# The transposes of the masked LoRA values: from TensorE to VectorE

## What is computed

```
x = x + S4(x)                    # a long convolution, masked by a length
x = x + einsum(x, W1[cond])      # per-sample 32x32 channel mixes
x = x + einsum(x, W2[cond])
def lora_add(base, inp, A, B):
    t = einsum('bri,bni->bnr', A[idx], inp)
    return base + einsum('bor,bnr->bno', B[idx], t) * 0.5
gate = lora_add(x @ W_gate.T, x, A_gate, B_gate)
up   = lora_add(x @ W_up.T,   x, A_up,   B_up)
act  = silu(gate) * up
x = x + lora_add(act @ W_down.T, act, A_down, B_down)
```

## Time and profile before

| | us |
|---|---|
| median of 3 runs | 1084.07 (1083.23 to 1085.55) |
| the profiled execution | 1087.87 |
| its span, first to last instruction | 1086.1 |
| PE busy | 1054.7 (97%) |
| DVE, ACT, POOL busy | 264.7, 405.2, 484.8 (24%, 37%, 45%) |
| mean granted clock of PE | 0.997 of full speed |

### The profile page before, as it was taken

One profiled execution on the slowest core, in us unless ns is written; L12 is line 12 of the kernel. 1 busy time (PEld: TensorE's weight loads), 2 busy tenths in 40 slices (PEclk: granted clock), 3 DMA queues, 4 the chain that ended last, 5 costly groups with the idle time before them and its releaser, 6 DMA issues.

```text
span 1086.1 us, 18858 instructions
## 1 busy us (share of the span) xinstructions
PE 1054.7 (97%) x6136; PEld 928.8 (86%) x6136; DVE 264.7 (24%) x519; ACT 405.2 (37%) x627; POOL 484.8 (45%) x301
## 2 busy tenths in 40 slices
PE   3899899999999999999999999999999999999998
PEld 3665699888889899998898998999888889989997
DVE  8333112222222222222221222122222212221222
ACT  7002234434433443343344334333434433343341
POOL 0604355445445444545454454445454544544441
PEclk9999999999999999999999999999999999999999
DMA  9699442424333333424243333434242433334320
GB/s 342 220 397 333 127 115 92 133 59 140 92 111 101 104 108 101 120 85 133 64 135 97 108 99 99 119 100 117 83 133 69 135 94 105 100 99 123 102 74 20
DMA packets 100979, 135.49 MB, mean 125 GB/s; under 512 B 26395, under 2 KB 59420, under 8 KB 100956
## 3 DMA queue, kind: packets, MB, share of 16 engines
q1 hardware_dynamic: 100380, 135.12, 40.3%
q10 hardware_dynamic: 576, 0.08, 0.1%
HBM read 118.11 MB, written 16.99 MB: 124 GB/s over the span
## 4 chain that ended last, share of the span: by engine, by line
PE 93%; DMA 3%; DVE 2%; SPq 1%; issue 0%; ACT 0%; DVEq 0%
PE ps L959 45%; PE ps L1001 26%; PE ps L969 7%; PE ps L931 5%; PE ps L990 4%; DMA tr<-kpad 1%; PE ps L949 1%; DMA x1p<-yo 1%; PE ps L1024 1%; PE ps L1023 1%; PE ps L941 1%; PE ps L942 1%; PE ps L944 1%; PE ps L977 1%; SPq L208 0%
## 5 line engine op out<-in xcount | busy, mean ns | idle before, releaser
L959 PE MATMUL ps<-wg_hi,x_hi 128*128 128x512 f32 (+2 forms) x768 | 296.3, 386 | 0.4 <-DVE x_lo L799 0.4
L959 PE MATMUL ps<-wg_lo,x_hi 128*128 128x512 f32 (+2 forms) x768 | 290.7, 378 | 0.0
L959 PE MATMUL ps<-wg_hi,x_lo 128*128 128x512 f32 (+2 forms) x768 | 290.6, 378 | 0.0
L468 POOL TENSOR_TENSOR bst<-braw,bst 128x1024 fp32r<-128x1024 f32 (+1 forms) x96 | 213.0, 2219 | 112.7 <-ACT bst L567 112.7
L959 PEld LDWEIGHTS ps<-wg_hi,x_lo 128*128 128x128 f32 x768 | 144.5, 188 | 25.5
L583 ACT ACTIVATE at_hi<-ps 128x512 fp32r<-128x512 f32 (+1 forms) x95 | 53.4, 562 | 300.1 <-PE ps L990 298.6
L959 PEld LDWEIGHTS ps<-wg_hi,x_hi 128*128 128x128 f32 x768 | 144.9, 189 | 22.5 <-issue 0.6
L959 PEld LDWEIGHTS ps<-wg_lo,x_hi 128*128 128x128 f32 x768 | 144.8, 189 | 21.6
L1001 PE MATMUL ps<-wd_hi,at_hi 128*128 128x288 f32 x696 | 153.5, 302 | 0.0
L1001 PE MATMUL ps<-wd_hi,at_lo 128*128 128x288 f32 x696 | 149.1, 296 | 0.0
L1001 PE MATMUL ps<-wd_lo,at_hi 128*128 128x288 f32 x696 | 148.6, 295 | 0.0
(11 more groups left out here) (150 smaller groups left out, 1104.9 us busy)
## 6 DMA issues: line engine op xcount, KB each, us to landing
braw<-in_tb SPq DMA_DIRECT2D x256, 128.0 KB, 2.7
braw<-in_tb SPq DMA_DIRECT2D x128, 96.0 KB, 2.4
adraw<-in_tad SPq DMA_DIRECT2D x128, 88.0 KB, 2.0
tr<-kpad SPq DMA_DIRECT2D x16, 512.0 KB, 6.7
x1p<-yo SPq DMA_DIRECT2D x16, 512.0 KB, 5.6
xb<-in_x SPq DMA_DIRECT2D x32, 256.0 KB, 2.9
agraw<-in_ta SPq DMA_DIRECT2D x128, 64.0 KB, 2.0
bdraw<-in_tbd SPq DMA_DIRECT2D x128, 64.0 KB, 2.2
```

Source lines behind the costliest of these rows:

```text
L468: sub(v, b_from(p, q), v.bitcast(F32), ALU.subtract).then_inc(s["blo"], 1)
L959: last = mm(bank[:, 0:n], x3s[a][:, k, :], wgs[b][:, k, o:o + n], start=(k == 0 and a + b == 0), stop=False, skip_group_check=True)
```

## The change

`t_turn` and `td_turn` move from the program of PE to that of DVE. There each is one `transpose` instruction, which transposes each 32x32 block where it stands; since `tm` and `tdm` have nothing outside the blocks of the diagonal, this is the transpose of the whole. It writes a new SBUF buffer, `tr2` (128 x 256) or `tdr` (128 x 128), in place of `misc` in PSUM. Each waits first for the semaphore of the mask instruction right ahead of it, and raises the semaphore that PE's transpose raised. `t_high`, `t_low`, `td_high` and `td_low` read the new buffers. PE does neither transpose and waits for neither `tm` nor `tdm`. Nothing else is moved.

```
+        tr2 = sb("tr2", [P, 2, P])
...
+        tdr = sb("tdr", [P, P])
...
             def t_high(t):
                 act.wait_ge(s["tmt"], t + 1)
-                copy(ts2[0][:].rearrange("p u n -> p (u n)"), misc[:, 0:2 * P], ACT.Copy).then_inc(s["thi2"], 1)
+                copy(ts2[0][:], tr2[:], ACT.Copy).then_inc(s["thi2"], 1)
...
-                copy(tds[0][:], misc[:, 0:P], ACT.Copy).then_inc(s["tdhi"], 1)
+                copy(tds[0][:], tdr[:], ACT.Copy).then_inc(s["tdhi"], 1)
...
+            def t_turn(t):
+
+                dve.wait_ge(s["tm"], t + 1)
+                V.transpose(tr2[:].rearrange("p u n -> p (u n)"), tm[:].rearrange("p u n -> p (u n)")
+                            ).then_inc(s["tmt"], 1)
+
+            def td_turn(t):
+                dve.wait_ge(s["tdm"], t + 1)
+                V.transpose(tdr[:], tdm[:]).then_inc(s["tdt"], 1)
+
             def t_low(t):
                 dve.wait_ge(s["thi2"], t + 1)
-                tt(ts2[1][:].rearrange("p u n -> p (u n)"), misc[:, 0:2 * P],
-                   ts2[0][:].rearrange("p u n -> p (u n)").bitcast(F32), ALU.subtract).then_inc(s["tlo2"], 1)
+                tt(ts2[1][:], tr2[:], ts2[0][:].bitcast(F32), ALU.subtract).then_inc(s["tlo2"], 1)
...
-                tt(tds[1][:], misc[:, 0:P], tds[0][:].bitcast(F32), ALU.subtract).then_inc(s["tdlo"], 1)
+                tt(tds[1][:], tdr[:], tds[0][:].bitcast(F32), ALU.subtract).then_inc(s["tdlo"], 1)
...
                 t_mask(t, p)
+                t_turn(t)
                 if not first:
                     a_low(t - 1, 2)
                 t_low(t)
                 if not first:
                     td_mask(t - 1, 1 - p)
+                    td_turn(t - 1)
                 act_mul(t, p, 0)
...
-            def t_turn(t):
-                pe.wait_ge(s["tm"], t + 1)
-                for u in range(2):
-                    last = nc.tensor.transpose(misc[:, u * P:(u + 1) * P], tm[:, u, :], ident)
-                last.then_inc(s["tmt"], 1)
-
-            def td_turn(t):
-                pe.wait_ge(s["tdm"], t + 1)
-                nc.tensor.transpose(misc[:, 0:P], tdm[:], ident).then_inc(s["tdt"], 1)
...
                 chunk(p, 0, 1)
-                t_turn(t)
                 if not first:
                     down(t - 1, 1 - p, 2)
...
                 chunk(p, 1, 0)
-                if not first:
-                    td_turn(t - 1)
                 a_turn(t, 0)
```

More of the change, by code:

```diff
@@ L882, in _ @@
             td_mask(NT - 1, 1)
+            td_turn(NT - 1)
             td_low(NT - 1)
@@ L1086, in _ @@
             down_half(0, range(j0, j0 + 2))
-            td_turn(NT - 1)
             down_half(0, range(j0 + 2, j1))
```

## The result

| | us |
|---|---|
| before, median of 4 runs | 1084.81 (1083.23 to 1085.56) |
| changed, median of 4 runs | 1075.26 (1074.38 to 1075.70) |
| ratio | 0.9907, 95% interval 0.9887 to 0.9927 |
| the profiled execution of the changed kernel | 1074.99, span 1073.2 |

The changed kernel is faster by 0.9%, 9.6 us; the prediction was 10.6 us and 1073.5, with a range of 1071.0 to 1076.8. Of the 1.8 us between 1073.5 and 1075.26, 0.7 are the median before, which is 1084.81 here and was 1084.07 when the prediction was made; 1.0 is the gain itself.

The account below looks back on a forecast made before the run. PE's own instructions were taken to bound every tile but the first; 7.1 (`t_turn`) + 3.5 (`td_turn`) + 0 (first tile) = 10.6 us less, 1084.07 to 1073.5 us, range 1071.0 to 1076.8.

Parts of the forecast that it names:

- PE bounds every tile but the first: In the other 31 tiles PE waits for nobody, so what leaves its program shortens the tile.
- `t_turn`, 0.23 us: Last chunk matmul to second row of `down`: 0.65 to 0.42 us, 0.23 less in 31 tiles, 7.1 us.
- `td_turn`, 0.11 us: Head of the transposes of `a_turn` on PE: 0.11 us less, 32 times, 3.5 us.
- The sum, 10.6 us: Whole kernel: 7.1 + 3.5 + 0 = 10.6 us less, from 1084.07 to 1073.5 us.
- The slow start behind transposes, 0.09 us: At `down` on PE: of the 0.23 us, 0.14 are the two transposes and 0.09 a slow start behind them.
- the rival, by which 0.09 of it stays: At `down`: the slow start has another cause and stays, 2.8 us less gain, 1076.3 us; chance 7%.
- The first tile gives nothing: First tile: PE arrives sooner but waits longer for `act_mul`, which hangs on a DMA; 0, with 1.5 us to both sides.
- DVE's transpose costs what a plain instruction costs: On DVE: 0.43 us for `t_turn`, 0.29 for `td_turn`; the first may last 0.94 us at no cost.
- the rival had the right mechanism: Dear DVE transpose, 1.7 us for 256 elements, makes PE wait in 31 tiles: +13.0 us, 1097.1; chance 5%.
- `t_high` and `td_high` as long from SBUF as from PSUM: Instructions reading the transposes: same lengths from SBUF as from PSUM, with slack of microseconds.
- Transposes at their full records, 26 us: On PE: 96 transposes cost 0.271 us each, so 26.0 us go, 1058.1 us; chance 2%.
- POOL: `b_low` on POOL holds DVE up at `t_turn` in every second tile: 15 us lost, 1088 us; chance 2%.

Follow-up runs that it names:

- only_t: Changed kernel with the transpose of `tdm` left on PE, only those of `tm` on DVE; 1080.09 us, ratio 0.9950 to the kernel before.
- only_td: Changed kernel with the two transposes of `tm` left on PE, only that of `tdm` on DVE; 1082.91 us, ratio 0.9974 to the kernel before.
- dup_old: Changed kernel plus two unused PE transposes of the identity where `t_turn` was, ahead of `down`; 1084.19 us, ratio 0.9980 to the kernel before.
- dup_row: Changed kernel plus two unused PE transposes at the head of the transposes of `a_turn(t, 0)`; 1081.75 us, ratio 0.9960 to the kernel before.
- first_sp: Changed kernel, SP issuing the first tile's loads of B for piece 1 before reading the first block's indices; 1073.11 us (one execution).
- dve_plus2: Changed kernel plus two further unused transposes of `tm` on DVE ahead of the used one; 1081.49 us, ratio 0.9954 to the kernel before.
- dve_plus1: Changed kernel plus one further unused transpose of `tm` on DVE ahead of the used one; 1076.16 us (one execution).
- dve_plus3: Changed kernel plus three further unused transposes of `tm` on DVE ahead of the used one; 1091.39 us, ratio 1.0051 to the kernel before.
- first_early: As first_sp, and POOL makes `b_low(0, 1)` ahead of `x_sum(1)` in the first tile; 1072.66 us, ratio 0.9877 to the kernel before.

## Why the prediction was right, point by point

- **PE bounds every tile but the first.** Right: everything done to PE's program moved the tile by its own size (0.213, 0.097, and back 0.213, 0.197), and PE waits for nobody in the loop of the changed kernel.
- **`t_turn`, 0.23 us.** Nearly right: 0.213 (`only_t`). The 0.65 to 0.42 us is exactly there. Slightly less arrives, since the rest of `down` is slower by 0.016 us in 24 matmuls than behind the transposes. The split of the 0.23 was wrong, see the slow start below.
- **`td_turn`, 0.11 us.** 0.097 (`only_td`).
- **The sum, 10.6 us.** This is the term that was mis-sized: 0.34 per tile, where the tiles gave 0.303. Of the 0.037, 0.003 is rounding (the means over 28 tiles are 0.229 and 0.108), and 0.034 is given back as slightly longer distances between PE's matmuls behind the places of the transposes: 0.016 in `down(t-1, 2)`, and 0.018 behind `td_turn`'s place, most of it in `lora_b(t, 1)` and `chunk(2, 0)`. What makes these some nanoseconds slower no run shows. From the last `tm` to the end 0.5 us went, where 0.45 were counted (one `t_turn`, two `td_turn`).
- **The slow start behind transposes, 0.09 us.** Wrong as a mechanism, without harm to the sum. `dup_old` shows that the 0.213 us come and go with the transposes, so the rival, by which 0.09 of it stays, is out. But the weight loads put each transpose at 0.108 us there too, 0.22 for the two, and `dup_old` against `dup_row` leaves 0.017 for the change of kind. The recorded start of `down`, from which 0.14 and 0.09 were split, is early. That the sum of both was right is because it ended at the second row of `down`, beyond that record.
- **The first tile gives nothing.** Right: 0.12 us less, and two further profiles of the changed kernel have 30.98 and 31.18 against 30.94 before. The wait moved to `act_mul`, and `first_sp` shows that this hung on the load.
- **DVE's transpose costs what a plain instruction costs.** Right: 0.445 for 0.43, 0.311 for 0.29. The room for it was put at 0.94 us, which is some 0.07 too much (0.90 - 0.03 = 0.87 by the estimate from `dve_plus2`), as the weight load of `down` was left out. That changed nothing, for 0.445 is well inside: `dve_plus1` is free, `dve_plus2` costs 0.125 us a tile, `dve_plus3` is slower than before. So the rival had the right mechanism, and the instruction did not reach the threshold. The figure of 311 ns in the Trainium skill, page "VectorE: DVE Perf Modes", section "The three transpose paths", given there for bf16, is what fp32 takes here.
- **`t_high` and `td_high` as long from SBUF as from PSUM.** Wrong, in slack: 418 for 384 ns and 302 for 277 (last section). And `td_low` is held by POOL up to 648 ns.
- **Transposes at their full records, 26 us.** Wrong as a cost, as expected: of 271 ns a transpose costs PE some 108. The 275 ns of the Trainium skill, page "TensorE: Matmul & The Clock Gate", section "Part 4: PE-mode transpose", agree with the length of the record, 271 ns, and not with this cost.
- **POOL.** It holds DVE up, but not at the transposes, and hidden; the last section has the rows.

## What to carry to other kernels

When PE bounds and is never idle, even a cheap instruction taken from it counts, at its distance from start to start. Read that over a stretch that ends well beyond it: the total from chunk to the second row of `down` was right, while the recorded start of the first row was 0.08 us off. Before an instruction is put into another engine's order, add that engine's idle time at the place and the time that its next result lies ready unused; the sum is the free room, less what the reader must do first (here a weight load, 0.11 us), and beyond it each microsecond is paid in every tile. A mask that leaves only 32x32 blocks on the diagonal makes the cheap block transpose a full one.

## What the runs showed of the hardware

**POOL holds a DVE instruction with two SBUF inputs, not the transpose.** `td_low` read one input from PSUM before (291 to 292 ns, always). From SBUF it is (ns min/median/max):

```profile
L846 DVE TENSOR_TENSOR td_lo<-tdr,td_hi x32: 283/286/648, 157.2 to 1068.9; 128x128 fp32r<-128x128 f32 x32
```

It is long in 14 of the 32 tiles, every second one of the loop, there where `b_low` runs. DVE, then POOL, in such a tile:

```profile
541.47 0.31 DVE L819 STREAM_TRANSPOSE tdr<-tdm 128x128 f32<-128x128 f32 x1
...
542.72 0.63 DVE L846 TENSOR_TENSOR td_lo<-tdr,td_hi 128x128 fp32r<-128x128 f32 x1
```

```profile
540.80 2.40 POOL L470 TENSOR_TENSOR bst<-braw,bst 128x1024 fp32r<-128x1024 f32 x1
```

POOL ends at 543.20 and `td_lo` at 543.35, though it began at 542.72; in all 14 such tiles it ends 0.15 us behind POOL. The transpose at 541.47 lies wholly within POOL's instruction and takes its usual 311 to 314 ns, as in the other 13. The Trainium skill, page "SBUF — State Buffer", section "SBUF: two separate sides", has it that of a VectorE instruction with two SBUF inputs and a GpSimd one that reads SBUF the later is blocked until the other has ended; the 14 tiles agree. Here it costs nothing: PE wants `td_lo` microseconds later.

**ACT reads SBUF a little slower than PSUM here.** `t_high` went from 384 to 418 ns, `td_high` from 277 to 302 (means of 32); nothing waits for the difference.

**The stretch at the lower clock in the first tile varies.** About the end of PE's wait and behind it, the granted clock in the changed kernel is 0.50 of full speed, 1.2 GHz (busy (x) of PE, PEld, DVE, ACT, POOL; PEclk, DMA share, GB/s):

```profile
129.00:130.00 1.00, 1.00 (x4) 0.81 (x4) 0.26 (x1) 0.49 (x1) 1.00 (x1) 0.50 0.45 126
```

That lasts some 3 us, as it did before, with the wait 1.2 us longer. In `only_t`, with a wait of 3.8 us, it lasted about 7 us, from 126.8, ahead of the wait's end, to 133.6, and its first tile took 1.24 us more than the changed kernel's. In `first_early`, which has no wait at this place, every microsecond from 128 to 137 was granted in full; so was every one from 126 to 140 in `first_sp`, with its wait of 2.1 us, while in the kernel before it fell at one of 2.3 us. The 1.24 us are of the size of the 1.5 that the prediction allowed for this; why `only_t` stays low twice as long no run shows.
